# VectorE's order within a step: both score maxima first, layernorm and weight work last

## The reference

```python
x = x + attention(layernorm(x))
x = x + ffn(layernorm(x))
# attention: rms_norm with gamma, qkv = xn @ w_qkv (16 heads of 64),
#   softmax(q k^T / 8) v per head, then @ w_out (1024 -> 256)
# ffn: gelu(x @ w1 + b1) @ w2 + b2 (256 -> 1024 -> 256), times the sum of the
#   two normalised top router probabilities of 8 experts
```

## Time and profile before

| what | value |
|---|---|
| median of 3 runs | 1256.65 us (1254.92 to 1259.24) |
| the profiled execution | 1257.61 us |
| its span | 1255.8 us, 29276 instructions |
| TensorE (PE) busy | 1199.8 us |
| VectorE (DVE) busy | 967.2 us |
| ScalarE (ACT) busy | 901.0 us |
| GpSimd (POOL) busy | 642.5 us |
| mean granted clock of TensorE | 0.99 |

### The profile page before, as it was taken

One profiled execution on the slowest core, in us unless ns is written; L12 is line 12 of the kernel. 1 busy time (PEld: TensorE's weight loads), 2 busy tenths in 40 slices (PEclk: granted clock), 3 DMA queues, 4 the chain that ended last, 5 costly groups with the idle time before them and its releaser, 6 DMA issues.

```text
span 1255.8 us, 29276 instructions
## 1 busy us (share of the span) xinstructions
PE 1199.8 (96%) x11354; PEld 1060.0 (84%) x11354; DVE 967.2 (77%) x1736; ACT 901.0 (72%) x1925; POOL 642.5 (51%) x799
## 2 busy tenths in 40 slices
PE   7889999999999999999999999999999988999998
PEld 6778888888888888888888888888888877888887
DVE  5688788878887888788878887888788864666654
ACT  4777888788878887788778877888888783244432
POOL 3555465546555555556555555556465665222221
PEclk9899999999999999999999999999999999999999
DMA  4122111311131113111311131113111231111100
GB/s 153 35 51 68 35 35 36 85 36 35 35 85 35 36 35 85 34 36 35 84 37 34 36 85 36 35 35 85 35 35 35 69 83 40 68 38 64 35 17 34
DMA packets 31657, 62.92 MB, mean 50 GB/s; under 512 B 5664, under 2 KB 7968, under 8 KB 31520
## 3 DMA queue, kind: packets, MB, share of 16 engines
q1 hardware_dynamic: 31520, 61.05, 19.0%
HBM read 19.08 MB, written 8.39 MB: 22 GB/s over the span
## 4 chain that ended last, share of the span: by engine, by line
PE 70%; DVE 12%; ACT 7%; POOL 5%; issue 4%; DMA 1%; SPq 0%; DVEq 0%; POOLq 0%; ACTq 0%
PE ps L429 36%; PE ps L487 14%; PE ps L473 9%; PE ps L445 7%; ACT prob L712 5%; DVE pT_lo L891 4%; DVE negmax L959 4%; PE ps L449 3%; POOL prob L792 2%; DVE nat L891 1%; ACT nat L679 1%; POOL wbig_lo L836 1%; DMA wstage<-in_w_qkv 1%; POOL att_hi_v L812 1%; POOL attT_lo L818 1%
## 5 line engine op out<-in xcount | busy, mean ns | idle before, releaser
L792 POOL TENSOR_SCALAR prob<-prob,rowinv 128x512 f32<-128x512 f32 x512 | 349.3, 696 | 349.2 <-DVE rowinv L964 348.7
L712 ACT ACTIVATE prob<-ps,negmax 128x512 f32<-128x512 f32 x512 | 347.6, 686 | 55.0 <-DVE negmax L959 50.9
L891 DVE TENSOR_TENSOR pT_lo<-ps,pT_hi 128x512 fp32r<-128x512 f32 (+1 forms) x384 | 320.2, 862 | 31.1 <-ACT pT_hi L703 13.0
L959 DVE TENSOR_REDUCE negmax<-ps 128x2 f32<-128x1024 f32 x256 | 309.4, 1208 | 1.1 <-PE ps L449 1.1
L473 PEld LDWEIGHTS ps<-identity,prob 64*128 64x128 f32 x4096 | 160.8, 140 | 96.4 <-POOL prob L792 57.3
L473 PE MATMUL ps<-identity,prob 64*128 64x64 f32 x4096 | 180.7, 227 | 40.0 <-POOL prob L792 16.1
L700 ACT ACTIVATE pT_hi<-ps 128x1024 fp32r<-128x1024 f32 x128 | 131.5, 1027 | 109.5 <-issue 105.3
L445 PE MATMUL ps<-nat 64*128 64x512 f32 x1024 | 178.0, 418 | 1.4 <-DVE nat L891 1.4
L487 PE MATMUL ps<-pT_hi,vbuf 128*128 128x256 f32 x1024 | 164.9, 283 | 1.2 <-DVE pT_lo L891 1.2
L487 PE MATMUL ps<-pT_lo,vbuf 128*128 128x256 f32 x1024 | 164.6, 283 | 0.0
L487 PEld LDWEIGHTS ps<-pT_hi,vbuf 128*128 128x128 f32 x1024 | 145.2, 190 | 7.6 <-DVE pT_lo L891 1.9
(11 more groups left out here) (111 smaller groups left out, 2281.4 us busy)
## 6 DMA issues: line engine op xcount, KB each, us to landing
att_hi_v<-halves_out SPq DMA_DIRECT2D x128, 128.0 KB, 2.3
att_lo_v<-halves_out SPq DMA_DIRECT2D x128, 128.0 KB, 2.3
xin<-in_x SPq DMA_DIRECT2D x8, 512.0 KB, 3.8
xres<-in_x SPq DMA_DIRECT2D x8, 512.0 KB, 3.5
x_scratch<-xres SPq DMA_DIRECT2D x8, 512.0 KB, 3.1
out_y<-f_o SPq DMA_DIRECT2D x16, 256.0 KB, 2.1
prob<-in_w_qkv SPq DMA_DIRECT2D x5, 512.0 KB, 4.9
wstage<-in_w SPq DMA_DIRECT2D x4, 512.0 KB, 3.9
```

Of the source, the lines that this page charges most:

```text
L712: act.activation(prob[:, n % NPROB, j * SEQ:(j + 1) * SEQ], ps[:, PS_SCORE[n % 2] + j, :], ACT.Exp, bias=negmax[:, n % 4, j:j + 1], accum_ ...
L792: return pool.tensor_scalar(dst, src, scalar, 1.0, ALU.mult, ALU.mult)
L891: return dve.tensor_tensor(dst, full, hi, ALU.subtract)
L959: dve.tensor_reduce(negmax[:, n % 4, :], ps[:, PS_SCORE[n % 2]:PS_SCORE[n % 2] + 2, :], AX.X, ALU.max, negate=True).then_inc(s_max, 1)
```

## The change

Within a step, VectorE now takes the maximum of the odd tile directly after the low part of the even tile's transposes, then the even tile's reciprocal, then the low part of the first aux block, and the work of both slots last. Before, the even slot's work came first, then the reciprocal, the odd maximum, the first aux block and the odd slot's work. Nothing else differs; the other engines keep their order.

```diff
                     row_max(2 * step)
                 if 0 <= 2 * step - 2 < NUNIT:
                     transposed_lo(2 * step - 2)
-                slot_tasks(2 * step)
+                if 0 <= 2 * step + 1 < NUNIT:
+                    row_max(2 * step + 1)
                 if 0 <= 2 * step < NUNIT:
                     row_inverse(2 * step)
-                if 0 <= 2 * step + 1 < NUNIT:
-                    row_max(2 * step + 1)
                 for block_of_aux in aux_of(step)[0]:
                     aux_done(*block_of_aux)
+                slot_tasks(2 * step)
                 slot_tasks(2 * step + 1)
```

## The result

The changed kernel takes 1235.29 us (median of four runs, 1232.66 to 1239.76) against 1257.06 (1254.92 to 1259.24) for the kernel before in the same session: ratio 0.9836, 95% interval 0.9817 to 0.9855. The profiled execution of it took 1239.76, of which 1238.0 is its span; it is the slowest of the four, so its trace shows 17.8 us less than the span of before (1255.8).

The account below looks back on a forecast made before the run. TensorE, busy for 96% of the span, was taken as the bound, so only its idle time could be won. Terms summed to 10.95 us gained, from the shown median 1256.65 to 1245.7; the range was 1240.0 to 1252.0.

Parts of the forecast that it names:

- (a): Start of step 9: the q low part comes 1.6 us sooner and eight TensorE stalls go wholly, 8.7 us gained.
- (b): Start of step 10: the v low part comes 0.8 us sooner; six stalls go and sequence 0's shrinks, 3.4 us gained.
- (d): Clock in sequence 0: the half-speed stretch of TensorE after the 1.87 us stall disappears, 1.45 us gained.
- (f): Step 14: the v low part comes 0.4 us sooner, but ScalarE holds the second stall; 1.0 us gained.
- the change fills half of these waits: VectorE's waits for exponentials before reciprocals, 132.7 us: the even tile's half is filled, so they fall to about half.
- term (c): Steps 9 and 10: scale and normalisation run beside GpSimd's multiplication, and the delay becomes new TensorE stalls, 4.5 us lost.
- no cost by contention: Rival: GpSimd and VectorE meet only briefly or the late reciprocal has slack, so 15.5 us gained, 1241.2; chance 0.22.
- Term (e): Other places in sequence 0: gains after step 7 and in step 1, first scores 0.4 us later; 1.25 us gained.
- VectorE's work is only shifted: Rival: in steps 8 to 11 the stalls reappear ahead of even tiles' transposes, leaving 3.3 us gained, 1253.3; chance 0.10.
- the even tile late: Slower rival: the even reciprocal behind the maximum delays 64 even tiles' transposes, 19.2 us lost, 1264.9; chance 0.04.

Follow-up runs that it names:

- e2: Against the changed kernel: the even slot's work goes back ahead of everything, so only the odd maximum moves ahead of the even reciprocal; 1247.16 us, ratio 0.9929.
- e3: Against the changed kernel: the even reciprocal goes back ahead of the odd maximum, so only the slot work moves last; 1243.45 us, ratio 0.9898.
- e10: Against e7: VectorE writes the first transposed input block's high part itself at the end of step 13, not waiting for ScalarE; 1226.23 us, ratio 0.9783.
- e7: Against the changed kernel: ScalarE splits the early weight pieces in sequence 0 behind the odd exponentials; 1231.59 us, ratio 0.9807.
- e9: Against the changed kernel: the second layernorm scaling is left out for sequences 1 to 7; 1232.52 us in a single execution.
- e5: Against the changed kernel: VectorE does the layernorm's scale twice in step 9, for the layernorms of sequences 1 to 7; 1239.64 us, ratio 0.9875.
- e1: The changed kernel timed again without any edit; 1233.57 us, ratio 0.9820 to the kernel before.
- e4: Against the changed kernel: the even reciprocal also goes behind the first aux block's low part; 1234.69 us, ratio 0.9821.
- e6: Against the changed kernel: GpSimd multiplies the even tile ahead of the attention output in even steps; 1237.78 us, ratio 0.9853.

## Why the prediction was wrong

**Direction, places and stalls were right.** TensorE idles at the starts of steps 9 and 10 because of what stands ahead of a low part on VectorE. Terms (a) and (b) measured 9.3 and 4.1 against 8.7 and 3.4, (d) 1.46 against 1.45, (f) 1.6 against 1.0. The half-speed stretch at about 103 us is missing from every trace in which the slot work goes last, and stands in e2's, where it doesn't. e3, which moves the slot work alone, gains 12.8 us. That ScalarE holds the second stall of step 14 is shown by e10.

**The first step that failed** is the sentence "In all steps without slot work nothing is gained: TensorE has no gap there". I took "no idle time printed" for "no wait". Each odd step hid 0.15 us behind the ends of the last matmuls, each even step 0.03 to 0.05. e2, in which no slot work moves, gains 8.9 us; in the two profiled traces these steps give 3.7 and step 13 another 0.47 a sequence, of which part is given back in step 14. The cause: ahead of the v low part stood a reciprocal that waits for the even exponentials, and then the maximum of 1.21, so the low part came that wait later. Behind the maximum the same reciprocal finds its exponentials done (no idle time in front of 547.26). That is what filling the reciprocals' waits is worth here, and I had set it at nothing. (e2 moves the odd maximum and the v low part forward together; that it is the low part which counts is read from the rows, where the transposes start 0.11 us after its end.) The reading "the change fills half of these waits" was wrong too, as said above: the even tile's waits were 31.6 of the 132.7 us.

**The second is term (c), mis-sized**: -4.5 forecast, -0.7 measured. Its mechanism is there, in all sequences. The scale's second operation, all eight of it, before (duration in ns, minimum, median and maximum):

```profile
L881 DVE TENSOR_SCALAR ln_norm<-ln_norm x8: 169/170/171, 8.5 to 855.3; 128x4 f32<-128x4 f32 x8
```

In the changed kernel:

```profile
L881 DVE TENSOR_SCALAR ln_norm<-ln_norm x8: 171/648/653, 8.4 to 840.6; 128x4 f32<-128x4 f32 x8
```

The four operations together take 1.37 us (593.68 to 595.05) where they took 0.80 (604.26 to the reciprocal at 605.06), so VectorE did lose about 0.6 us in step 9, as I had said. What failed is "VectorE has no idle time to spare in steps 9 and 10". The rows of before already held some, behind the scale, and I had looked only at the 0.92 us ahead of it. VectorE of before, the reciprocals of steps 9 and 10:

```profile
607.86 0.17 DVE L964 RECIPROCAL rowinv<-rowsum 128x2 f32<-128x2 f32 x1 [0.21 <-ACT prob L712]
...
612.43 0.17 DVE L964 RECIPROCAL rowinv<-rowsum 128x2 f32<-128x2 f32 x1 [0.22 <-ACT prob L712]
```

These two waits are 0.43 us, and shorter gaps that print nothing come on top. TensorE's steps 9 and 10 of sequence 4 as windows (columns as in e7), before:

```profile
598.85:607.08 8.23, 7.77 (x84) 7.12 (x85) 6.92 (x15) 6.61 (x18) 4.01 (x5) 1.00 0.02 4
607.08:614.59 7.51, 7.48 (x72) 6.47 (x73) 6.88 (x12) 6.09 (x15) 5.16 (x6) 1.00 0.56 151
```

And in the changed kernel:

```profile
586.59:594.16 7.57, 7.57 (x85) 6.98 (x84) 7.24 (x17) 6.46 (x16) 4.70 (x7) 1.00 0.00 1
594.16:601.82 7.66, 7.66 (x73) 6.23 (x72) 7.55 (x16) 5.95 (x14) 5.39 (x7) 1.00 0.69 196
```

Length less busy time, VectorE was idle for 1.31 and 0.63 us in these two steps before, and for 0.33 and 0.11 after. The odd reciprocal (595.70) and the even one behind it (600.68) now wait for nothing. So the delay of 0.6 ran into idle time, and only 0.15 to 0.19 a sequence came out as a stall, by e9. e3 says the same from the other side. Its reciprocal comes a maximum earlier, so that GpSimd is done before the scale begins, and nothing is drawn out there:

```profile
L881 DVE TENSOR_SCALAR ln_norm<-ln_norm x8: 170/171/171, 8.8 to 846.2; 128x4 f32<-128x4 f32 x8
```

Yet its step 10 is 7.58 us long, 0.08 more than its plain even steps; that of the changed kernel is 7.62, 0.15 more than its own. The rival "no cost by contention" (1241.2, a chance of 0.22) had the size right and the kind of reason, a wait in front of a reciprocal, though it named another one; its second reason came true as well, since the copy behind the statistics takes 0.53 us in the mean of sequences 1 to 6 instead of 0.78. It too lacked the hidden waits, and so it also lies above what was measured. e5 shows where the reserve ends: beyond it each 0.8 us costs 0.8.

**Term (e)** came out at -0.7 in this trace, against 1.25 forecast, and at 0.3 in e1's; its size is in part chance. Step 2 of sequence 0 became 1.05 us longer, as the half-speed stretch there took 6.8 us instead of 3.4 (the 0.57 of the window above). Step 11 of sequence 0 went from 7.72 to 8.48, since the attention output waited 2.13 us for its transfer and held the even tile's multiplication (7.78 in e1). What the term named for step 7 came true, 0.47 us against 0.45.

**The other rivals.** That VectorE's work is only shifted is refuted by steps 8 to 11: 32.10 us together before, 30.27 after. The slower rival, the even tile late: e4 finds no measurable cost in delaying its reciprocal further. A trace of it remains in the scattered stalls, 1.3 us before and 3.2 after, and e6 shows their way: a late transfer holds the attention output, and that holds the multiplication behind it.

**What stays open**: how much of the 4.5 us between the profiled execution of the changed kernel and its median comes from the half-speed stretches. Step 2 of sequence 0 alone differs by 2.6 us between executions (last section), but no trace was taken of the fastest runs of the changed kernel. Whether the scattered stalls of a single execution are chance or set by the order of transfers wasn't tried either.

## What to carry to other kernels

An engine at 96% without printed gaps can still be waiting in every round of its loop: compare the distance between the starts of the same instructions in different rounds, and the end of the low part or copy that releases them, before writing "nothing to gain". Where a short instruction waits for another engine and a long one behind it is ready, try the long one first; here that gained 8.9 us. And price an added delay by all the idle time of that engine behind it, printed or not, in the order that the change makes, and not by whether the engine looked full before.

## What the hardware showed that was not expected

**A tiny VectorE operation can wait out a GpSimd instruction.** An operation on 4 columns takes 170 ns alone and 648 in the median behind the start of a GpSimd multiplication: it began at 593.95 and ended at 594.60, and the two multiplications, 1.37 us from 593.21, ended at 594.58. The Trainium skill (SBUF — State Buffer, section "SBUF: two separate sides") describes the port pair that the two engines share as an exclusive lock, held for the whole instruction; this row agrees. The same section limits this to VectorE operations in a 2-port mode or with two inputs in SBUF, a condition that the prediction left out. The v low part, with one input in PSUM, took its usual 0.74 us beside the same multiplications. In these rows the cost goes by what is left of the other engine's instruction and not by the size of VectorE's own: 0.48 us for 4 columns here, 0.31 and 0.56 for two operations on 256 columns (1.04 and 1.29 instead of 0.73).

**Equal stalls don't always cost the clock.** The stretches of half speed (granted clock 0.5, the lower of its two levels) in sequence 0 began, in the profiled executions, at 14.4, 34.9, 51.9, 69.0 and 103.1 us before, at 12.8, 33.3, 53.7 and 70.8 in the changed kernel, and at 14.7 alone in e7; each took 3.4 or 6.8 us. In the changed kernel both stalls of 1.85 us were followed by one; in e5 the one behind step 3 was not (its step 4 is 7.50 long instead of 9.01). And step 2, behind a stall of 2.85 us, is 10.09 long in the changed kernel and 7.49 behind one of 2.84 in e9. Both e5 and e9 are the changed kernel's program up to step 9 of sequence 0. So executions of the same instructions can differ by 1.5 or 2.6 us at one such place, with the same stall in front.
